# Warm-up on bare zeros, other places for the mixing moves, five subtracts on TensorE, last copies split by strip

## What is computed

```
out   = einsum('oi,nikj->nokj', g_weight, patches(x));  cen = out + x
for shift in (1, 3):
    prod = conv(cen, k1, shift) * conv(cen, k2, shift)   # 4 directions per channel
    outs.append(min(prod, axis=direction))
out   = max(outs) + mean(outs)
g     = pointwise(depthwise3x3(out, dw), pw)
return cen * sigmoid(g) + cen
```

## Time and profile before

| | us |
|---|---|
| median of 3 runs | 115.16 |
| lowest and highest | 113.99, 115.18 |
| the profiled execution's own time | 115.35 |
| its span in the profile | 113.5 |

### The profile page before, as it was taken

One profiled execution on the slowest core, in us unless ns is written; L12 is line 12 of the kernel. 1 busy time (PEld: TensorE's weight loads), 2 busy tenths in 40 slices (PEclk: granted clock), 3 DMA queues, 4 the chain that ended last, 5 costly groups with the idle time before them and its releaser, 6 DMA issues.

```text
span 113.5 us, 2311 instructions
## 1 busy us (share of the span) xinstructions
PE 88.3 (78%) x918; PEld 42.6 (38%) x918; DVE 88.6 (78%) x126; ACT 54.8 (48%) x90; POOL 85.9 (76%) x77
## 2 busy tenths in 40 slices
PE   2697979999999079699795499758189949938980
PEld 1196957667776033143221122213021314312250
DVE  5121596995959895565999999999999959799941
ACT  4101554565556653336728580697391391430930
POOL 6400799999999999999999969999992059880400
PEclk9999999999999955899999679999976999999999
DMA  3999000000000499300009832004995000897043
GB/s 50 387 304 370 17 6 0 6 0 6 3 6 0 84 167 236 107 0 0 0 5 223 247 114 98 0 0 92 251 249 182 0 0 0 225 286 263 0 165 118
DMA packets 5722, 12.11 MB, mean 107 GB/s; under 512 B 816, under 2 KB 1616, under 8 KB 5584
## 3 DMA queue, kind: packets, MB, share of 16 engines
q1 hardware_dynamic: 4976, 10.47, 32.6%
q10 hardware_dynamic: 736, 1.49, 4.1%
HBM read 3.18 MB, written 2.10 MB: 47 GB/s over the span
## 4 chain that ended last, share of the span: by engine, by line
DVE 24%; POOL 23%; PE 23%; ACT 9%; DMA 7%; issue 7%; ACTq 3%; SPq 1%; DVEq 0%; POOLq 0%
POOL u L222 22%; PE acc L734 9%; PE acc L784 6%; DVE m L620 6%; DVE slots L609 6%; ACT slots L522 4%; DMA early<-in_first_dram 4%; DMA early<-att 3%; DVE att L634 3%; PE acc L697 2%; PE slots L784 2%; ACTq L561 2%; PE slots L697 2%; DVE att L626 2%; DVE early L673 2%
## 5 line engine op out<-in xcount | busy, mean ns | idle before, releaser
L222 POOL TENSOR_TENSOR u<-cen 128x1056 f32<-128x1056 f32 (+9 forms) x44 | 70.6, 1651 | 7.9 <-DVE u L222 7.9
L522 ACT ACTIVATE slots<-u 128x1024 f32<-128x1024 f32 (+2 forms) x48 | 35.2, 744 | 30.7 <-POOL u L222 16.4
L609 DVE TENSOR_TENSOR slots<-slots,u 128x1024 f32<-128x1024 f32 (+2 forms) x36 | 30.8, 871 | 8.7 <-ACT slots L522 8.5
L784 PE MATMUL acc<-early,wc 128*32 128x512 f32 x168 | 22.1, 675 | 8.0 <-DMA early<-att 8.0
L713 PE MATMUL acc<-early 128*32 128x256 f32 (+1 forms) x512 | 24.8, 353 | 1.4 <-DVE cen L598 0.7
L620 DVE TENSOR_TENSOR m<-slots,m 128x1024 f32<-128x1024 f32 (+2 forms) x30 | 25.8, 860 | 0.1
L713 PEld LDWEIGHTS acc<-early 128*32 128x32 f32 x512 | 18.3, 110 | 7.7 <-issue 1.3
L784 PEld LDWEIGHTS acc<-early,wc 128*32 128x32 f32 x168 | 5.4, 120 | 24.3 <-issue 14.3
L689 PE MATMUL acc<-eye 128*128 128x512 f32 x22 | 11.4, 652 | 3.8 <-POOL eye L437 2.2
L755 PE MATMUL slots<-m,eye 128*128 128x512 f32 x24 | 11.8, 614 | 3.1 <-ACT m L537 3.1
L606 DVE TENSOR_TENSOR m<-slots,u 128x1024 f32<-128x1024 f32 (+2 forms) x12 | 10.3, 862 | 2.8 <-ACT slots L522 2.7
(11 more groups left out here) (39 smaller groups left out, 56.1 us busy)
## 6 DMA issues: line engine op xcount, KB each, us to landing
early<-att SPq DMA_DIRECT2D x24, 204.0 KB, 3.6
early<-in_x_dram SPq DMA_DIRECT2D x1, 1024.0 KB, 5.7
out_dram<-early SPq DMA_DIRECT2D x2, 512.0 KB, 5.3
early<-eye SPq DMA_DIRECT2D x1, 816.0 KB, 6.9
early<-att ACTq DMA_DIRECT2D x4, 204.0 KB, 5.0
early<-in_g_weight_dram SPq DMA_DIRECT2D x1, 768.0 KB, 7.4
out_dram<-early SPq DMA_DIRECT2D x3, 256.0 KB, 2.6
early<-in_first_dram ACTq DMA_DIRECT2D x2, 320.0 KB, 5.0
```

What stands on the lines that cost most here:

```text
L222: return eng.tensor_tensor(u[j][:, r0 - base:r1 - base, g], cen[:, PAD + r0:PAD + r1, g, left:left + wide], cen[:, PAD + r0 - dy:PAD + r1 ...
L522: nc.scalar.activation(slot_px(j, t), ahead(j, t), ACT.Copy).then_inc(u_copied, 1)
L609: nc.vector.tensor_tensor(slot_px(j, t), slot_px(j, t), here(j, t), ALU.mult).then_inc(multiplied, 1)
L784: last = nc.tensor.matmul(at[C * q:C * (q + 1)], weights[:, i, :], src[:, y0:y0 + r1 - r0, :, i:i + W], start=i == 0, stop=i == TAPS - 1)
```

## The change

- **Warm-up.** The zeroed part of `eye` is its first 512 columns, with a semaphore count of its own; the identity moves behind them. TensorE's warm-up, now two matmuls, waits for those zeros only, and so does ScalarE's first sigmoid.
- **Mixing moves.** Moves 2, 3, 4 and 6 stand behind other copies: after (0,2), (0,4), (1,0) and (1,6) instead of (0,1), (0,3), (1,1) and (1,7).
- **Subtracts.** (1,4) goes from POOL to DVE. (4,1), (5,1) and (5,5) go from POOL to TensorE as differences 2, 3 and 4. Difference 2 stands ahead of strip 1: four passes into bank 0 of acc, then, when the gate of strip 0 has left bank 1, four into that. Differences 3 and 4 (384 columns, one bank each) stand ahead of strip 3, when the gate of strips 1 and 2 is done. Strips 1 and 3 wait for ScalarE's moves of them, which stand after (3,6) and (4,4).
- **Warm-up ahead of strips.** None ahead of strip 1 (was 2), one ahead of strip 3 (was 3).
- **Gates and results.** The gate of strip 0 is after (3,4) instead of (3,6). POOL's third result is after (5,7) instead of (5,4).
- **Last copies.** The rows of stage 5 are cut by the strip that reads them. For strip 7: four parts of 272 columns on DVE, three of 136 on ScalarE, one of 136 on POOL. For strip 8: five of 272 on DVE, three of 272 and one of 136 on ScalarE, three of 136 on POOL. Each engine does strip 7's first, and strip 7 waits for those alone.

```diff
--- before.py
+++ after.py
...
-    DVE_SUBTRACTS = [(0, 0), (0, 4)]
-    PE_SUBTRACTS = [(3, 5), (4, 5)]
-
-    MOVE_AFTER = {(0, 1): 2, (0, 3): 3, (1, 1): 4, (1, 3): 5, (1, 7): 6, (2, 0): 7, (2, 2): 8, (2, 4): 9}
-    DIFFERENCE_AFTER = {(2, 6): 0, (2, 7): 1}
-    GATE_AFTER = {(3, 6): 0, (4, 1): 1, (4, 7): 2}
+    DVE_SUBTRACTS = [(0, 0), (0, 4), (1, 4)]
+    PE_SUBTRACTS = [(3, 5), (4, 5), (4, 1), (5, 1), (5, 5)]
+
+    MOVE_AFTER = {(0, 2): 2, (0, 4): 3, (1, 0): 4, (1, 3): 5, (1, 6): 6, (2, 0): 7, (2, 2): 8, (2, 4): 9}
+    DIFFERENCES_AFTER = {(2, 6): [0], (2, 7): [1], (3, 6): [2], (4, 4): [3, 4]}
+    DIFFERENCES_BEFORE_STRIP = {1: [2], 3: [3, 4]}
+    GATE_AFTER = {(3, 4): 0, (4, 1): 1, (4, 7): 2}
     KEEP_AFTER = {3: 0, 4: 0, 5: 1}
...
     POOL_UNITS = 3
-    RESULT_AFTER = [(4, 1), (4, 6), (5, 4)]
+    RESULT_AFTER = [(4, 1), (4, 6), (5, NP - 1)]
     OWN_AFTER = {(0, 3): (1, 2), (0, NP - 1): (2, HP)}
...
-    WARM_BEFORE_X = 1
+    WARM_BEFORE_X = 2
     WARM_BEFORE_SUM = {}
-    WARM_BEFORE_STRIP = {1: 2, 3: 3, 5: 5}
+    WARM_BEFORE_STRIP = {3: 1, 5: 5}
     ACT_WINDOWS = {(5, 2): [(5, 2), (5, 3)], (5, 5): [(6, 2), (6, 3)]}
...
         m3 = sb("m3", [P, G * K * W])
-        eye = sb("eye", [P, (2 * WP - 1) * P])
+        eye = sb("eye", [P, BANK + P])
         minus = sb("minus", [P, P])
...
+        def difference_px(i):
+
+            t, j = PE_SUBTRACTS[i]
+            r0, r1 = u_new(j, t)
+            at = BANK * (i % 2) if r1 - r0 <= SR else 0
+            return acc[:, at:at + (r1 - r0) * G * W]
+
         def first_mixed(w):
...
-        PARTS = QUADS * TAPS
-        DVE_LAST, ACT_LAST, POOL_LAST = range(0, 6), range(6, 10), range(10, PARTS)
-
-        def last_part(n, early_rows=False):
-
-            q, dy = divmod(n, TAPS)
+        EARLY_PARTS = [(q, dy, *rows) for q in range(QUADS) for dy, rows in enumerate(((0, 2), (0, 1), (3, 4)))]
+        PARTS_OF = {LAST: [(q, 2, 0, 2) for q in range(QUADS)] + [(q, 1, 1, 2) for q in range(QUADS)],
+                    LAST + 1: [(q, dy, 2, 4) for dy in range(2) for q in range(QUADS)]
+                              + [(q, 2, 2, 3) for q in range(QUADS)]}
+        DVE_PARTS, ACT_PARTS, POOL_PARTS = ({LAST: PARTS_OF[LAST][a:b], LAST + 1: PARTS_OF[LAST + 1][c:d]}
+                                            for a, b, c, d in ((0, 4, 0, 5), (4, 7, 5, 9), (7, 8, 9, 12)))
+
+        def last_part(q, dy, a, b):
+
             first = SR * LAST + dy
-            y0, y1 = max(0, S_ROWS[T - 1][0] + 1 - first), min(SR, H + 1 - first)
-            return [(window[2][C * dy:C * (dy + 1), q, G * AW * a:G * AW * b],
-                     att[C * q:C * (q + 1), first + a:first + b].rearrange("p y g x -> p (y g x)"))
-                    for a, b in ([(0, y0), (y1, SR)] if early_rows else [(y0, y1)]) if b > a]
-
-        EARLY_PARTS = sum(len(last_part(n, early_rows=True)) for n in range(PARTS))
+            return (window[2][C * dy:C * (dy + 1), q, G * AW * a:G * AW * b],
+                    att[C * q:C * (q + 1), first + a:first + b].rearrange("p y g x -> p (y g x)"))
...
-        ACT_PARTS = [part for parts in ACT_WINDOWS.values() for part in parts]
+        ACT_ISSUES = [part for parts in ACT_WINDOWS.values() for part in parts]
...
                 for q in range(QUADS):
-                    if (s, q) not in ACT_PARTS:
+                    if (s, q) not in ACT_ISSUES:
                         sp.dma_start(window[s % 2][0:TAPS * C, q], window_source(s, q)
...
-            nc.gpsimd.memset(eye[:], 0.0).then_inc(eye_zeroed, 1)
-            pool.wait_ge(eye_zeroed, 1)
-            mid = eye[:, (WP - 1) * P:WP * P]
+            nc.gpsimd.memset(eye[:, 0:BANK], 0.0).then_inc(eye_zeroed, 1)
+            mid = eye[:, BANK:BANK + P]
+            nc.gpsimd.memset(mid, 0.0).then_inc(eye_zeroed, 1)
+            pool.wait_ge(eye_zeroed, 2)
             nc.gpsimd.affine_select(out=mid, in_=mid, compare_op=ALU.not_equal, fill=1.0, base=0,
...
             pool.wait_ge(gated_pool, POOL_UNITS)
-            n_copied = 0
-            for n in range(PARTS):
-                for dst, src in last_part(n, early_rows=True):
-                    if n_copied:
-                        pool.wait_ge(part_copied, n_copied)
-                    nc.gpsimd.tensor_copy(dst, src).then_inc(part_copied, 1)
-                    n_copied += 1
+            for n, part in enumerate(EARLY_PARTS):
+                if n:
+                    pool.wait_ge(part_copied, n)
+                nc.gpsimd.tensor_copy(*last_part(*part)).then_inc(part_copied, 1)
             pool.wait_ge(att_ready, n_att(T - 1))
-            for n in POOL_LAST:
-                for dst, src in last_part(n):
-                    pool.wait_ge(part_copied, n_copied)
-                    nc.gpsimd.tensor_copy(dst, src).then_inc(part_copied, 1)
-                    n_copied += 1
+            for n, part in enumerate(POOL_PARTS[LAST] + POOL_PARTS[LAST + 1]):
+                pool.wait_ge(part_copied, len(EARLY_PARTS) + n)
+                nc.gpsimd.tensor_copy(*last_part(*part)).then_inc(part_copied, 1)
...
                 act.dma_start(chunk[k], first[:, k * CHUNK:(k + 1) * CHUNK]).then_inc(chunk_loaded[k], 16)
-            act.wait_ge(eye_ready, 1)
+            act.wait_ge(eye_zeroed, 1)
             nc.scalar.activation(warm_sigmoid[:], eye[:, 0:1], ACT.Sigmoid)
...
                 n_dve = len([p for p in DVE_SUBTRACTS if p <= (t, j)])
-                n_pe = len([p for p in PE_SUBTRACTS if p <= (t, j)])
                 if (t, j) in DVE_SUBTRACTS:
...
                 elif (t, j) in PE_SUBTRACTS:
-                    act.wait_ge(u_moved, n_pe)
+                    act.wait_ge(u_moved, PE_SUBTRACTS.index((t, j)) + 1)
                 else:
+                    n_pe = len([p for p in PE_SUBTRACTS if p <= (t, j)])
                     act.wait_ge(u_ready, NP * t + j + 1 - n_dve - n_pe)
...
                 act.wait_ge(subtracted, i + 1)
-                nc.scalar.activation(u[j][:, r0:r1].rearrange("p y g x -> p (y g x)"), acc[:],
+                nc.scalar.activation(u[j][:, r0:r1].rearrange("p y g x -> p (y g x)"), difference_px(i),
                                      ACT.Copy).then_inc(u_moved, 1)
...
                         move_mixed(MOVE_AFTER[t, j])
-                    if (t, j) in DIFFERENCE_AFTER:
-                        move_difference(DIFFERENCE_AFTER[t, j])
+                    for i in DIFFERENCES_AFTER.get((t, j), []):
+                        move_difference(i)
                     if (t, j) in GATE_AFTER:
...
             act.wait_ge(stored[1], 16)
-            for n in ACT_LAST:
-                for dst, src in last_part(n):
-                    last = nc.scalar.activation(dst, src, ACT.Copy)
-            last.then_inc(last_window_act, 1)
+            for strip in (LAST, LAST + 1):
+                for part in ACT_PARTS[strip]:
+                    last = nc.scalar.activation(*last_part(*part), ACT.Copy)
+                last.then_inc(last_window_act, 1)
             for i in range(len(GATE_AFTER), len(UNITS)):
...
                 nc.vector.tensor_tensor(att_px(t), slot_px(NP - 1, t), packed(m3, t), ALU.min).then_inc(att_ready, 1)
-            for n in DVE_LAST:
-                if n == DVE_LAST[0]:
-                    dve.wait_ge(att_ready, n_att(T - 1))
-                    dve.wait_ge(stored[1], 16)
-                for dst, src in last_part(n):
-                    last = nc.vector.tensor_copy(dst, src)
-            last.then_inc(last_window_dve, 1)
+            dve.wait_ge(att_ready, n_att(T - 1))
+            dve.wait_ge(stored[1], 16)
+            for strip in (LAST, LAST + 1):
+                for part in DVE_PARTS[strip]:
+                    last = nc.vector.tensor_copy(*last_part(*part))
+                last.then_inc(last_window_dve, 1)
             for i in range(POOL_UNITS, len(UNITS)):
...
         def _(pe):
-            pe.wait_ge(eye_ready, 1)
+            pe.wait_ge(eye_zeroed, 1)
...
             warm(WARM_BEFORE_X, acc[:, 0:BANK])
-            ident = eye[:, (WP - 1) * P:WP * P]
+            ident = eye[:, BANK:BANK + P]
+            pe.wait_ge(eye_ready, 1)
             for k in range(WP):
...
                 r0, r1 = u_new(j, t)
+                at = difference_px(i)
                 if i == 0:
                     pe.wait_ge(minus_ready, 1)
+                elif i <= 2:
+                    pe.wait_ge(u_moved, i)
                 else:
-                    pe.wait_ge(u_moved, i)
+                    pe.wait_ge(gate_ready, 2)
                 for b, r in enumerate(range(r0, r1, SR)):
+                    if i == 2 and b == 1:
+                        pe.wait_ge(gate_ready, 1)
+                    rows = min(SR, r1 - r)
                     for weights, y in ((ident, PAD + r), (minus, PAD + r - dy)):
-                        last = nc.tensor.matmul(acc[:, b * BANK:(b + 1) * BANK], weights[:],
-                                                cen[:, y:y + SR, :, PAD:PAD + W], start=weights is ident,
```

(18 more changed lines are left out.)

## The result

The changed kernel took 110.49 us (median; 110.11 to 112.96 over its runs), the kernel before beside it 114.93 us. The ratio of their times is 0.9617, with a 95% interval of 0.9538 to 0.9696: 4.4 us faster. The forecast was 109.4, a gain of 5.9 us; the time lies in its range, the gain is three quarters of the forecast one.

A forecast was written before the change was run, and what follows sets the result against it. POOL's subtracts, then TensorE's two differences until 54.07 us, then DVE were taken to bound the kernel. Terms 4.9 - 0.5 + 1.3 + 0.2 = 5.9 us off 115.35 gave 109.4, range 107.5 to 113.3.

The forecast's parts named there:

- What bounds the kernel: Whole kernel: POOL up to 38.69 us, TensorE's two differences until 54.07, then DVE; time won before 54.07 is kept.
- Start: Kernel start: earlier, longer warm-up raises the clock some 3 us earlier; 1.8 us gained for cen's first pieces and POOL's start.
- Subtract (1,4): Stage 1: moving this subtract from POOL to DVE puts POOL 0.65 us ahead net, bounds 0.4 and 1.15.
- Places of the moves: Mixing: swapped moves cost nothing, covered by POOL; move 6 loses about 1.1 us of DVE's stage 1, also covered.
- The hole: TensorE's wait ahead of the first two differences shrinks from 3.50 to 1.6 us, so the clock stays at 2.4 GHz.
- a sign of being wrong: Ahead of the differences: the prediction is wrong if TensorE's hole there passes 2.5 us.
- Rival A: Clock rises no earlier at the start; 2.9 us hole, differences at 1.2 GHz; 113.3 us, chance 0.2.
- Difference 2: Plane (4,1) on TensorE between strips 0 and 1: two holes may lower the clock; 0.5 us loss, bounds 0 and 1.7.
- The third result behind (5,7): Stage 5: three POOL subtracts go ahead of a gate it waited for; costed at nothing, bounds 0 and 0.3 gain.
- Strips 3 and 4: Shorter TensorE holes: 5.4 instead of 7.09 us, third gate 1.7 earlier, DVE's idle before stage 5 gone; 1.3 us gain.
- Last copies: Stage 5's end: split copies let strip 7 start sooner, until strip 6 holds TensorE; 0.2 us gain, bounds 0 and 0.3.
- tail: End of the kernel: the split of the last copies, forecast to gain 0.2 us.

The follow-up runs named there:

- the one with both additions: Changed kernel plus three warm-up matmuls ahead of the differences and two of strip 4's windows on ScalarE's queue: 109.22 us, kernel before 114.66.

## Why the prediction was right, and where it was too high

**What bounds the kernel** stood: all that was won ahead of stage 3 (3.86 us) reached stage 4 (3.86) and the end.

**Start, forecast 1.8, measured 0.69 in the profile.** The mechanism was right, and its size varies from execution to execution. The clock was forecast to rise 3 us earlier; in the changed kernel's profile it rose some 1.6 earlier (chunk groups step by 0.44 from 7.22 us on, before from 8.9), while in four of the eleven profiles with the new warm-up the groups step by 0.44 from the first one on. Over the eleven profiles of kernels with the new warm-up, DVE's first copy starts at 8.78 to 10.10 us, 9.34 on average; in the three with the old one at 10.51 to 10.96, 10.75 on average. So it is worth 1.4 us on average, 0.7 here: two chunk groups still ran at 1.2 GHz, the rest at 2.4. The range for it (0 to 1.9) held; one execution was read as if it were all of them. That x may cap the start of pieces 2 and 3 was real: in three profiles with the copy near 9.0, piece 2 waited to 11.1 to 11.5 for x.

**Subtract (1,4), forecast 0.65 for POOL, measured 0.67.** The estimate that POOL gives back 0.5 us was right: its add beside DVE's subtract took 0.98, without it 0.46, and the POOL subtract behind DVE's (1,4) takes 1.90 where the same one takes 1.42 in the kernel before. What I left out is the other direction. DVE's subtract starts at 23.03, while a POOL subtract runs until 23.79, and ends 0.6 behind that: 1.36 us instead of 0.73. Over the ten profiles with this subtract on DVE it took 1.35 to 1.37 in seven, 1.89 in one, where a POOL subtract of 1.41 us had just begun, and 0.73 in the two in which POOL's ended about 0.1 us behind its start. DVE had the time.

**Places of the moves, forecast 0, measured 0.** The microsecond of DVE's stage 1 that move 6 was to cost did not appear either: DVE has no idle time ahead of its product of (1,7).

**The hole, forecast 1.6, measured 3.08: the step that failed.** POOL was 1.33 us ahead at (2,4) instead of 2.45 (the start's 1.1 is the difference), and TensorE's mixing ended at 36.0 instead of 36.35. The hole hardly shrank, and it passed the 2.5 us that the prediction had named as a sign of being wrong. The clock stayed high all the same, so the term came out nearly as forecast, by luck and not for the forecast's reason: holes of this length leave it high in some executions and not in others. Holes of 3.08, 3.16 and 3.17 us (the changed kernel twice, the one with three differences undone) left it, holes of 3.05, 3.21, 3.51 and 3.64 did not. Rival A put it down as certain at 2.9 us, and was wrong in that. The gain at stage 3 adds up from the profile: start 0.69, (1,4) 0.65, difference 0 2.83, less 0.31 because its move now waits behind copy (2,6): 3.86.

**Difference 2, forecast 0.5 of loss, measured 0.** Every time of the working stood within 0.3 us once shifted by 3.87. It also brings nothing, as the profile of the kernel without the three differences shows. The third result behind (5,7), forecast at nothing, was undone in that same kernel and made no difference either.

**Strips 3 and 4, forecast 1.3, measured 0.26: the second step that failed.** The clock did stay high (4.15 us from the start of strip 3 to that of strip 4 are a wait, not a low clock), but I took TensorE's end for the release of the third gate without asking what is late next. It is the windows of strip 4. SyncE issues eight transfers one behind the other from 73.03 to 79.11, and the last lands at 82.74, 1.2 us behind the end of strip 3. In the kernel before, TensorE was slow enough to hide that: its 7.05 us for the two strips have no idle time in them. Nor is the 0.26 shown to come from this edit, since the kernel without the new differences has it too. Moving two issues to another queue gave 0.7 us in DVE's stage 4, and 0.9 us of time. The rows of SyncE's queue, in the changed kernel and in the one with both additions:

```profile
73.03 6.08 SPq L429 DMA_DIRECT2D early<-att  x8
...
72.82 4.55 SPq L429 DMA_DIRECT2D early<-att  x6
```

**Last copies, forecast 0.2, profiles 0.3 to 0.6, times nothing that can be told.** The step was right: with the copies split, strip 6 and not the copies holds strip 7.

Together: 5.9 forecast; start 1.1 less, strips 3 and 4 1.0 less, difference 2 0.5 more, tail 0.2 more make 4.5, near the 4.6 of the spans.

## What to carry to other kernels

When a term rests on TensorE's clock, one profiled execution is one draw: price both cases, and if a hole of some 3 us lies ahead of matmuls on the critical path, fill it. Here that took two lines and was worth 2 us in the kernel before; in the changed kernel, where the clock fell in some executions only, the gain is likely but within the noise. When an engine on the path becomes faster, look up what else its consumer waits for (here the eighth of eight DMA issues on one queue) before the gain is booked.

## What the runs showed of the hardware that I had not expected

- POOL and DVE slow each other down when both subtract from SBUF, and it goes both ways: POOL's 128-column add took 0.98 us beside DVE's subtract and 0.46 with hardly any of it beside, DVE's 560-column subtract took 0.73, 1.36 or 1.89 us, by how much of a POOL subtract was still to run when it started. The Trainium skill (SBUF — State Buffer, section "SBUF: two separate sides") states that such a pair contends for a port that one of them holds for its whole instruction; the runs agree: DVE's subtract ends 0.6 us behind the end of POOL's.
- The length of a hole alone did not decide the clock. Ahead of the differences holes of 3.08, 3.16 and 3.17 us left it at 2.4 GHz and holes of 3.05 and 3.21 lowered it; ahead of strips 1 and 2 holes of 2.82 and 2.84 left it and 2.86 and 2.89 lowered it; ahead of strip 3 it fell behind all four holes of 2.75 to 2.84; at x it fell behind three of 2.18 to 2.54; and once it fell behind 1.37, 1.27 and 0.40 us with work between.
- The load of x (1024 KB) took 4.7 to 6.8 us from SyncE's issue to its landing over the fourteen profiles (4.7 in the one with strip 4's windows on two queues, 6.8 in the one with the moves at their old places), with the same loads beside it.
